# A fused adaLN-FFN kernel: step orders, a start of the Sinkhorn chains without a logarithm, and GpSimd blocks and gathers

## The reference, cut to what matters

```python
x = x + _L0_ffn_ref(_L0_cond_ref(x, W, ids), ...)      # einsum, then layernorm, int8 w1, gelu, int8 w3
y = einsum(x, weight) + bias + scale * lora(x)          # L1_cond
H_res = sinkhorn_log(rms(y) @ W_res.T + base)           # 4x4 a row, 50 iterations, tau = 0.1
H_pre, H_post = softmax(...), softmax(...)              # 4 each
x_pre = einsum("btnc,btn->btc", y_streams, H_pre)       # the gather
out = x + einsum(H_res, y_streams) + (x_pre @ W_branch) * H_post
```

## Time and profile before

| | us |
|---|---|
| median of 3 runs | 744.5 (744.49 to 746.52) |
| the profiled execution | 746.49 |
| its span in the trace | 744.6 |
| PE busy / DVE busy / ACT busy / POOL busy | 707.5 / 546.3 / 393.6 / 79.6 |
| granted PE clock, mean | 0.987 |

### The profile page before, as it was taken

One profiled execution on the slowest core, in us unless ns is written; L12 is line 12 of the kernel. 1 busy time (PEld: TensorE's weight loads), 2 busy tenths in 40 slices (PEclk: granted clock), 3 DMA queues, 4 the chain that ended last, 5 costly groups with the idle time before them and its releaser, 6 DMA issues.

```text
span 744.6 us, 10403 instructions
## 1 busy us (share of the span) xinstructions
PE 707.5 (95%) x3300; PEld 474.4 (64%) x3300; DVE 546.3 (73%) x1886; ACT 393.6 (53%) x676; POOL 79.6 (11%) x57
## 2 busy tenths in 40 slices
PE   8999999999999999999997999999999999969967
PEld 5445445656537565446655888888888887646755
DVE  4569676979742977775663437877999899999974
ACT  1255846666742574737445545354524645967322
POOL 0111400302030032642040000000000000000000
PEclk9999999999999999999999999999999999989998
DMA  7997255558734335852042303303032137666624
GB/s 296 410 410 293 95 196 193 193 171 298 279 136 144 128 129 177 320 193 103 33 155 84 128 1 128 114 15 128 1 129 81 48 140 256 202 203 218 219 92 141
DMA packets 52477, 124.35 MB, mean 167 GB/s; under 512 B 6211, under 2 KB 31939, under 8 KB 46920
## 3 DMA queue, kind: packets, MB, share of 16 engines
q1 hardware_dynamic: 51128, 120.96, 45.6%
q10 hardware_dynamic: 1296, 2.74, 1.0%
HBM read 97.96 MB, written 25.72 MB: 166 GB/s over the span
## 4 chain that ended last, share of the span: by engine, by line
PE 71%; DVE 19%; ACT 6%; issue 3%; DMA 1%; SPq 0%; ACTq 0%; DVEq 0%
PE PS L1044 18%; PE PS L1238 15%; PE PS L1121 13%; PE PS L1032 8%; DVE kprod L1772 4%; DVE ksum L1776 4%; PE PS L1053 2%; DVE ka L1779 2%; DVE kb L1779 2%; PE PS L1363 2%; PE PS L1155 2%; PE PS L1369 2%; PE PS L1226 2%; PE PS L1381 1%; DVE xp L1691 1%
## 5 line engine op out<-in xcount | busy, mean ns | idle before, releaser
L1044 PE MATMUL PS<-w_raw,x_raw 128*128 128x512 f32 x320 | 141.6, 595 | 1.2 <-DMA w_raw<-cond_w_dram 0.8
L1044 PEld LDWEIGHTS PS<-w_raw,x_raw 128*128 128x128 f32 x320 | 59.4, 190 | 69.5 <-issue 69.5
L1238 PE MATMUL PS<-w_hi,xT_hi 128*128 128x512 f32 x256 | 103.0, 402 | 0.0
L1238 PE MATMUL PS<-w_hi,xT_lo 128*128 128x512 f32 x256 | 100.8, 394 | 0.0
L1238 PE MATMUL PS<-w_lo,xT_hi 128*128 128x512 f32 x256 | 100.5, 393 | 0.0
L1776 DVE TENSOR_REDUCE ksum<-kprod 128x16 f32<-128x64 f32 x392 | 69.8, 212 | 2.5
L590 POOL TENSOR_TENSOR xres<-xres,vecs 128x1024 f32<-128x1024 f32 x16 | 42.2, 2655 | 218.7 <-DMA xres<-x_tok_dram 218.7
L685 ACT ACTIVATE qT<-PS,round_c 128x1024 bf16<-128x1024 f16 x32 | 35.5, 1109 | 56.4 <-PE PS L1053 56.4
L1121 PE MATMUL PS<-w3q,qT 128*128 128x512 bf16 x256 | 57.8, 379 | 1.0 <-ACT qT L685 1.0
L1121 PE MATMUL PS<-w1q,qT 128*128 128x512 bf16 x256 | 57.9, 379 | 0.3 <-ACT qT L685 0.3
L1238 PEld LDWEIGHTS PS<-w_hi,xT_lo 128*128 128x128 f32 x256 | 48.4, 189 | 10.5
(11 more groups left out here) (209 smaller groups left out, 1343.0 us busy)
## 6 DMA issues: line engine op xcount, KB each, us to landing
w_raw<-cond_w_dram SPq DMA_DIRECT2D x31, 1024.0 KB, 5.5
x_raw<-x_tr_dram SPq DMA_DIRECT2D x32, 256.0 KB, 6.4
stage<-w_dram SPq DMA_DIRECT2D x16, 512.0 KB, 16.6
xres<-x_tok_dram SPq DMA_DIRECT2D x8, 1024.0 KB, 8.2
x_scratch<-x1buf SPq DMA_DIRECT2D x16, 512.0 KB, 6.6
x1n<-x_scratch SPq DMA_DIRECT2D x16, 512.0 KB, 6.8
y_scratch<-y SPq DMA_DIRECT2D x16, 512.0 KB, 3.9
my<-y_scratch SPq DMA_DIRECT2D x12, 512.0 KB, 4.0
```

Source lines behind the costliest of these rows:

```text
L1044: mm = pe.matmul(PS[:, 2 * t + h, :], x_raw[pr][:, c, t * P:(t + 1) * P], w_raw[pr][:, c, h * H2:(h + 1) * H2], start=(pr == 0 and c == 0) ...
L1238: pe.matmul(PS[:, 2 * t + h, :], xx[:, c, t * P:(t + 1) * P], ws[c // 2][:, c % 2, h * H2:(h + 1) * H2], start=(c == 0 and xx is xT_hi and ...
```

## The change

Nothing of what is computed changes, apart from the chain's start: the normalisation of rows by a logarithm is replaced by an exponential of doubly shifted logits, row sums and a product, which gives the same matrix. The edits:

1. `FIRST` is (3, 2, 2): pairs 1 and 2 of sample 2 are split too (homes in `w_hi`).
2. The chain's start has no logarithm, so ScalarE has two exponentials and no table change in it.
3. GpSimd gathers tile 1 of every sample in three operations (L634, L638, L640 of the kernel after), VectorE tile 0; of sample 7 GpSimd gathers both. GpSimd also builds the blocks 1, 8, 9, 10 and 11.
4. The tables of shares change: 71 iterations stand in steps 2 to 7 where 67 stood.
5. TensorE's step has `base(b,0,1)` ahead of the transposes of `xp`, and `base(b,1,0)` ahead of `branch`; step 7 has neither those nor `select(0)`, which follow it. In the tail, `select(3)` follows `mix` of all 12 tiles and a second `keep_warm`.
6. The three operations of `finish` and the two of `pick` stand between the operations of an iteration of chain 3 alone (`beside`). Smaller ones: two swaps of `evac_T` and `gelu` on ScalarE, `x_transposes(1,0)` ahead of `low_and_heads(0)`, squares of y(7) taken by halves from PSUM.

```diff
-    FIRST = 3
+    FIRST = (3, 2, 2)
-        SHARES = {2: (3, 3, 3, 3), 3: (3, 3, 2, 4), 4: (2, 3, 3, 3), 5: (3, 3, 3, 3), 7: (3, 3, 4, 0)}
-        FIRST_REST, SECOND_SHARES = 2, (4, 4)
+        SHARES = {2: (2, 3, 3, 3), 3: (3, 3, 3, 4), 4: (2, 3, 3, 4), 5: (3, 3, 3, 3), 7: (4, 3, 3, 0)}
+        FIRST_REST, SECOND_SHARES = (1, 0), (2, 2, 4, 4)
...
+            def gather(b, tiles):
+                pool.wait_ge(hd_step, HD_OPS * (b + 1) + (b == NB - 1))
+                wait(pool, xpT_done, b)
+                prod = sq[:, :].rearrange("p (r c) -> p r c", r=NS)
+                for t in tiles:
+                    nc.gpsimd.tensor_tensor(prod, y[t][:, :].rearrange("p (r c) -> p r c", r=NS),
+                                            hp[:, NTOK * b + t, 0, :]...to_broadcast([P, NS, C]),
+                                            ALU.mult).then_inc(xp_at[t], 1)
+                    pool.wait_ge(xp_at[t], NS * b + 1)
+                    nc.gpsimd.tensor_tensor(sq[:, 0:H2], sq[:, 0:H2], sq[:, H2:D], ALU.add).then_inc(xp_at[t], 1)
+                    pool.wait_ge(xp_at[t], NS * b + 2)
+                    nc.gpsimd.tensor_tensor(xp[t][:, :], sq[:, 0:C], sq[:, C:H2], ALU.add).then_inc(xp_at[t], NS - 2)
...
+            lora_lo(0)
+            for b in range(NB - 1):
+                lora_lo(b + 1)
+                gather(b, (1,))
+            gather(NB - 1, range(NTOK))
+            for k in BY_POOL:
+                mix_block(k)
...
                 sk_link(nc.vector.tensor_tensor(sz, z, rows(s0, HG), ALU.subtract), 2)
+                sk_link(nc.vector.tensor_reduce(s1, sz.rearrange("p t i j -> p t j i"), AX.X, ALU.max), 3)
+                sk_link(nc.vector.tensor_tensor(kmat_t[c][:, :, :, :], sz, cols(s1, HG), ALU.subtract), 4)
                 between(0)
-                dve.wait_ge(sk_exp, 3 * c + 1)
...
+                dve.wait_ge(sk_exp, 2 * c + 1)
+                sk_link(nc.vector.tensor_reduce(s0, kprod[c][:, :, :, :], AX.X, ALU.add), 5)
+                sk_link(nc.vector.reciprocal(s1, s0), 6)
                 between(1)
+                dve.wait_ge(sk_exp, 2 * c + 2)
+                sk_link(nc.vector.tensor_tensor(hr, hr, rows(s1, HG), ALU.mult), 7)
...
             sinkhorn_start(3, beside_last_start)
-            gather_next(NB - 1, 3)
-            iterations(4, 1, 3)
+            pick(0)
+            lo_xp(NB - 2)
+            iterations(SINKHORN - 1 - done[1], 1, 3)
+            iterations(1, 3, beside=lambda i: finish_part(1, i))
+            iterations(BEFORE_LAST_LOW, 2, 3)
             lo_xp(NB - 1)
-            iterations(SINKHORN - 1 - done[1], 1, 3)
-            sinkhorn_finish(1)
-            iterations(6, 2, 3)
-            pick(1)
+            iterations(1, 2, 3)
+            iterations(1, 3, beside=lambda i: pick_part(1, i))
             iterations(SINKHORN - 1 - done[2], 2, 3)
-            sinkhorn_finish(2)
+            iterations(1, 3, beside=lambda i: finish_part(2, i))
             iterations(1, 3)
-            pick(2)
-            for k in BY_DVE[1:]:
-                mix_block(k)
+            iterations(1, 3, beside=lambda i: pick_part(2, i))
             iterations(SINKHORN - 1 - done[3], 3)
             sinkhorn_finish(3)
```

More of the change, by code:

```diff
@@ L911, in step_b @@
                 evac_y(b, 1)
-                if not last:
-                    evac_xT(b + 1, 1)
+                evac_xT(b + 1, 1)
                 square(b, 1)
@@ L916, in step_b, with step_last @@
                 head_exp(b)
+            def step_last(b):
+                stack_hi(b)
+                evac_ll(b)
+                for h in range(2):
+                    square_half(b, 0, h)
+                    evac_y_half(b, 0, h)
+                post_block(0, 0)
+                post_block(1, 1)
+                nc.scalar.activation(hd[:, 6, 0:1], round_c[:, 0:1], ACT.Sqrt)
+                square_half(b, 1, 0)
+                evac_y_half(b, 1, 0)
+                square_half(b, 1, 1)
+                head_root(b)
+                evac_y_half(b, 1, 1)
+                evac_xp(b - 1)
             act.wait_ge(b_ld, 16 * B_LOADS)
@@ L1292, in select, with step_b @@
                 mm.then_inc(hs_mm, 1)
-            def step_b(b, first=False, last=False):
+            def step_b(b, last=False):
                 base(b, 0, 0)
                 low_and_heads(b)
-                if last:
-                    select(0)
-                if not first:
+                base(b, 0, 1)
+                if not last:
                     branch_transposes(b - 1)
-                base(b, 0, 1)
                 low_rank(b, 0, 0)
                 low_rank(b, 0, 1)
-                if not first:
+                base(b, 1, 0)
+                if not last:
                     branch(b - 1)
-                base(b, 1, 0)
                 low_rank(b, 1, 0)
@@ L1389, in last @@
                 else:
-                    pe.wait_ge(nblk_done, len(BY_DVE) + i + 1 - sum(a < i for a in BY_ACT))
+                    pe.wait_ge(nblk_done, i + 1 - sum(a < i for a in BY_ACT))
                 pe.wait_ge(ny_ld[i], 16)
@@ L1418, in rest_only @@
                 rest_part(n, MIXED + i, nr[i], True)
-            mix(0)
-            mix(1)
+            branch_transposes(NB - 2)
+            select(0)
+            for k in range(2):
+                mix_rest(k)
+            branch(NB - 2)
+            for k in range(2):
+                mix_part(unit(k), k)
             rest_only(2, 0)
@@ L1424, in _ @@
             rest_only(3, 1)
+            select(1)
             branch(NB - 1)
@@ L1764, in _, with half @@
             done = [0] * CHAINS
-            def half(chains, row):
+            def half(chains, row, beside=None):
                 mat, vec, new = (kmat, kb, ka) if row else (kmat_t, ka, kb)
@@ L1773, in half @@
                                             ALU.mult).then_inc(k_step[c], 1)
+                if beside:
+                    beside(0 if row else 2)
                 for c, k in zip(chains, at):
@@ L1776, in half @@
                     nc.vector.tensor_reduce(ksum[c][:, :, :], kprod[c][:, :, :, :], AX.X, ALU.add).then_inc(k_step[c], 1)
+                if beside:
+                    beside(1 if row else 3)
                 for c, k in zip(chains, at):
@@ L1809, in share @@
                         iterations(SHARES[b][i], *((0,) if b < 4 else (0, 1) if b < 6 else (1, 2)))
-                    elif b == NB - 2 and i == 0:
-                        iterations(FIRST_REST, 0, 1)
-                        sinkhorn_finish(0)
-                    elif b == NB - 2 and i >= 2:
-                        iterations(SECOND_SHARES[i - 2], 1, 2)
+                    elif b == NB - 2:
+                        if i < 2 and FIRST_REST[i]:
+                            iterations(FIRST_REST[i], 0, 1)
+                            if done[0] == SINKHORN - 1:
+                                sinkhorn_finish(0)
+                        iterations(SECOND_SHARES[i], 1, 2)
                 lo_stacks(b)
-                if not first:
-                    lo_xp(b - 1)
                 if b in STARTS:
                     sinkhorn_start(STARTS[b], nothing)
-                if last:
-                    pick(0)
-                    mix_block(1)
                 share(0)
+                if not first and not last:
+                    lo_xp(b - 1)
                 share(1)
@@ L1860, in _ @@
+            def pick(c):
+                for i in range(2):
+                    pick_part(c, i)
             step_b(0, first=True)
```

304 lines of the change are left out of this document (170 added, 134 removed).

## The result

The changed kernel takes 757.24 us (median of 4 runs, 755.85 to 758.52) against 745.43 of the kernel before (4 runs): ratio 1.016, interval 1.0136 to 1.0181. It is slower by 12 us, where 7 were forecast. The profiled execution took 758.52, its span is 756.7; busy are PE 713.2, DVE 569.5, ACT 387.6 and POOL 123.3 us.

A forecast was written before the change was run, and what follows sets the result against it. Prediction: TensorE and VectorE level in steps 2 to 7, VectorE alone bounding the tail. Terms -4.2 + 13.0 + 4.2 - 5.8 = +7.2 us on 744.5 gave 751.7; own range 747 to 756, overall 736 to 760.

The forecast's parts named there:

- Upstream: Ahead of step 2: splits 0.9, ScalarE swaps 1.2 and part B's opening 2.1 us saved; -4.2 together, bounds -1 and -6.
- the opening of part B: Start of part B: the 1.6 us wait for `xT_lo` and PE's 0.5 wait for xp go, saving 2.1.
- Steps 2 to 7: Iterations +6.5, five gathers +15.5, three chain starts -6.5, step 7 -2.2: +13.3 us of VectorE work, taken as +13.0.
- My chain of turns: Gather in a step: VectorE's additions and GpSimd's operations alternate, so VectorE takes 6.0 us instead of 2.9, +3.1 a step.
- it all shows: Steps 2 to 7: the +13.3 us of VectorE work all lengthens the time, as VectorE had only 2 to 3 of waits.
- rival C: TensorE's new waits in the steps lower its clock: +2 to +6 us, 755 to 758; chance 0.14.
- The tail: Up to chain 3's end: savings of 1.2, 2.7 and 2.4 us against GpSimd's gathers and blocks, +7.6 and +2.9: +4.2.
- The 15 iterations behind `pick(2)`, 24 us, cover PE's 14 to 16 us for tiles 8 to 11: End of the tail: VectorE's 24 us of iterations after that pick hide TensorE's 14 to 16 us for tiles 8 to 11.
- The end: After chain 3: the last tiles start 3.0 us after `select(3)` starts, where 8.8 stood before: -5.8.
- the waits for `ls`: Sign in the profile after: TensorE waits on `ls` in most steps, over 8 us in total.
- Rival A: GpSimd's operations hardly hold VectorE up, since small ones pass; a gather costs 1.85 us, total 722; chance 0.12.
- Rival B: The lock is real but VectorE wins more turns: 4.3 us a gather, 4 in the tail; 737, half 744; chance 0.17.

The follow-up runs named there:

- the first experiment: The changed kernel with VectorE gathering both tiles of samples 0 to 6 as before, GpSimd keeping sample 7 and the five blocks: 743.06 us, ratio 0.9953.
- the two experiments that leave its part A alone: The kernel before with GpSimd's gather of tile 1 of samples 0 to 6 alone, 761.31 us; the kernel before with the chain's new start alone, 742.93 us.
- `f_end_transposes`: The changed kernel with 16 empty transposes added between the last selection and the last tiles: 754.91 us, ratio 1.0129.
- `sinkhorn_start` alone: The kernel before with only the chain's new start without logarithm: 742.93 us, ratio 0.9955.
- the table of before: The changed kernel with the old table of shares, 67 iterations in steps 2 to 7 instead of 71: 752.75 us, ratio 1.0095.

## Why the prediction was right, and where its sum was short

The forecast was slower, 751.7, its own range 747 to 756; the time is 757.2, a little above that and inside the range of 736 to 760. The mechanism was right: GpSimd's gather holds VectorE's up, and without it (the first experiment) the kernel takes 743. Several sizes of the sum were too large, a term was missing, and that the total came near is in part luck.

**Upstream, -4.2 forecast, -2.4 measured.** The first `lo_stacks` came 2.0 earlier (0.9 for the splits, 1.2 for the swaps: 2.1 forecast); no run here separates the two, and the kernel before itself has it at 402.4 in its profile and at 403.8 in those of the two experiments that leave its part A alone. The other 2.1, of the opening of part B, shrank to 0.5: the wait of 1.6 went, but a wait of 0.5 for the same tile came, and the first base behind it ran 6.7 instead of 5.7. In `f_end_transposes`, with the same wait, it ran 5.7, and the opening took 0.9 less.

**Steps 2 to 7, +13.0 forecast, +10.3 measured.** A gather costs 2.0 more than before and not 3.1: with five, 10.0 instead of 15.5. My chain of turns let GpSimd wait for each of VectorE's additions; it never did, since its next operation is issued 0.08 or 0.14 after the last, ahead of VectorE's. It let the first product pass as one of a single input, and that one waits as well. And GpSimd's product takes 1.9 and not 2.36. The other terms were off by the words "it all shows". A start is 2.8 or 2.9 instead of 4.85 or more, nearly as forecast, but three of them won 3.6 in the steps (`sinkhorn_start` alone), not 6.5. The four iterations cost 2.7 (the table of before against `f_end_transposes`), not 6.5. In the sum these two nearly cancel, which is luck. From `lo_stacks(2)` to `lo_stacks(7)` that makes 10.0 - 3.6 + 2.7 = 9.1, where `f_end_transposes` has 8.8 more than the kernel before. The changed kernel's profile has 12.4 more: the 3.6 between the two are TensorE's clock in step 6. Step 7 gave back 2.1 (2.2 forecast). The slow clock behind a wait is rival C's mechanism; it came beside the forecast and not in its place, and not in every profile.

**The tail, +4.2 forecast, +7.4 measured.** This is the step that failed. GpSimd's gathers of 7 and block 1 cost VectorE 3.5 instead of 7.6 (the late products add up to 1.0 + 0.57 + 1.16 + 0.54 + 0.26), since they are beside iterations, of which two operations in six wait. Its four other blocks cost 1.5 instead of 2.9. Both would have made the tail -1.3. But the sentence "The 15 iterations behind `pick(2)`, 24 us, cover PE's 14 to 16 us for tiles 8 to 11" looked only at TensorE's work behind that selection; the work ahead of it, from 637 on (eight tiles at 5.5 us, four rests, the `branch` products with their waits, 40 transposes), ends 10 us after chain 2: +9.0. That the four iterations more and the tighter list of VectorE bring chain 2's end forward, and TensorE's start back, was in my own figures; I never set the two against each other.

**The end, -5.8 forecast, -3.2 measured.** The last tiles start 2.8 us behind the start of `select(3)`, nearly as forecast (3.0). They then took 10.2 for 7.1 by the clock.

-2.4 + 10.3 + 7.4 - 3.2 = 12.1, the difference of the spans.

How much of the total was luck: the steps and the tail's GpSimd work were put 8 us too high, and a stall of 9.0 and 3.1 of slow clock at the end, which the sum didn't have, made up for it. An estimate from the measured terms: without those two the time would be about 757.2 - 9.0 - 3.1 = 745, no change at all. The time can't be put lower by this and may be higher, since TensorE has its own work in the tail: where the stall was cut from 9.0 to 3.0, the time fell by 4.5 and not by 6.

Of the marks to look for: the waits for `ls` (12.2, over 8 forecast), the last softmax at 636.2 (637), the last selection of 1.08 and the first addition at 1.47 are as forecast. GpSimd's rows L638 and L640 aren't stretched. Step 5 took 31.4, less than the 32 to 37 forecast, and step 6 40.8, more; in the three other profiles with the same list it took 37.1 to 38.4. Rival A falls: products of one and of two inputs do wait for GpSimd (2.08 for 0.35, 1.23 for 0.22). Rival B, fewer lost turns, was half right: a gather costs 4.9 and not its 4.3, but GpSimd's work in the tail costs 5.0, nearer to its 4 than to the forecast's 10.5.

## What to carry to other kernels

Work given to GpSimd beside a busy VectorE costs VectorE the rest of GpSimd's operation each time it issues one with two SBUF inputs, or a `tensor_scalar` as it is here (for two inputs only where GpSimd's operation reads SBUF too): count those starts, not the columns saved. A gather of 3 us on VectorE alone became 5 with half of it on GpSimd.

When a chain of small operations is threaded with steps that wait for another engine, put that engine's list beside it and ask at which time each of the two gets there, ahead of the wait as well as behind it; here 40 empty transposes fewer were worth 4.5 us, and one place in TensorE's list together with 16 transposes fewer 3.8.

An early finish is worth only what takes it up: iterations moved out of the tail were lost at a late selection.

Before a few microseconds between two profiles are given to an edit, look at the granted clock of the stretch in both, and at another profile with the same lists: here one step of the same list took 37.1 and 40.8.

## What was unexpected of the hardware

GpSimd's memset, which reads nothing, still held up a VectorE `tensor_scalar` while it ran (1.12 for the first and 0.69 for the second instead of 0.35, in all seven steps), but not the additions with two inputs (464 to 477 ns in all 42 rows).

GpSimd's product of 1024 columns with a broadcast operand takes 1.89 here, less than the 2.36 of the earlier trace rows, and a block of 512 columns, with both operands broadcast, 1.04 or 1.05, where 1.27 was taken. Whether it is the broadcast that makes them shorter was not tested.

The last tiles behind the same 1.75 us of idle TensorE took from 7.17 to 10.2 us in different kernels. The same holds for the wait of 3.2 us in step 6. The clock was lower behind such a stretch in some profiles and not in others; what else decides stays open.
